# Neighbour sums: one hand-over for four tiles instead of one for each, DMA landings relayed by ScalarE, and twelve products of zeros a group instead of sixteen

## What is computed

```python
def _gin_conv(x, src, dst, n, W1, b1, gamma, beta, W2, b2):
    agg = jax.ops.segment_sum(x[src], dst, num_segments=n)
    h = x + agg
    h = jax.nn.relu(_batchnorm(h @ W1 + b1, gamma, beta))
    return jax.nn.relu(h @ W2 + b2)
```

## Time and profile before

| | us |
|---|---|
| median of 3 runs | 7083.55 (7080.03 to 7084.12) |
| the profiled execution | 7078.6 |
| its span, first to last instruction | 7076.8 |
| first call of the helper, first DMA issue to end of the last add | 568.9 to 1140.6 |
| second call | 1237.7 to 1806.7 |
| third call | 6047.9 to 6622.5 |
| mean granted TensorE clock, whole span | 0.866 of 2.4 GHz |

### The profile page before, as it was taken

One profiled execution on the slowest core, in us unless ns is written; L12 is line 12 of the kernel. 1 busy time (PEld: TensorE's weight loads), 2 busy tenths in 40 slices (PEclk: granted clock), 3 DMA queues, 4 the chain that ended last, 5 costly groups with the idle time before them and its releaser, 6 DMA issues. The chain is left out here.

```text
span 7076.8 us, 95209 instructions
## 1 busy us (share of the span) xinstructions
PE 5214.7 (74%) x22994; PEld 3478.6 (49%) x22995; DVE 3522.3 (50%) x8494; ACT 1483.9 (21%) x3917; POOL 3388.5 (48%) x3530
## 2 busy tenths in 40 slices
PE   2767886888586788677852995799987459788645
PEld 0114554555334333366642884588864334455434
DVE  7994444444445566666662112566656232444312
ACT  0001002000232677611121221333333011000111
POOL 1636773777100676577733655366620110677222
PEclk8998998999797899878775997899998559999777
DMA  4103332333100000133321774233320223333245
GB/s 160 45 17 98 103 103 65 103 104 104 29 5 16 8 2 1 25 95 94 94 47 62 232 220 139 74 107 107 107 57 0 75 73 128 105 102 103 42 152 168
DMA packets 402836, 597.07 MB, mean 84 GB/s; under 512 B 130985, under 2 KB 305641, under 8 KB 401577
## 3 DMA queue, kind: packets, MB, share of 16 engines
q0 software_dynamic: 147584, 361.63, 18.9%
q1 hardware_dynamic: 255018, 232.69, 11.1%
HBM read 472.89 MB, written 121.17 MB: 84 GB/s over the span
## 5 line engine op out<-in xcount | busy, mean ns | idle before, releaser
L644 PE MATMUL ps<-wide 128*128 128x256 f32 x2640 | 906.5, 425 | 267.5 <-DMA wide<-table,src 139.1
L629 POOL DMA_INDIRECT wide<-table,src x880 | 855.6, 972 | 506.5 <-ACTq L94 239.1
L671 DVE TENSOR_TENSOR sums<-sums,ps 128x256 f32 x1320 | 555.4, 421 | 986.6 <-PE ps L644 982.8
L641 PE MATMUL ps<-zerow,zerob 128*128 128x256 bf16 x5280 | 797.6, 274 | 44.7 <-DVE wide L125 44.7
L644 PEld LDWEIGHTS ps<-wide 128*128 128x128 f32 x2640 | 396.1, 189 | 572.1 <-DMA wide<-table,src 375.4
L641 PEld LDWEIGHTS ps<-zerow,zerob 128*128 128x128 bf16 x5280 | 519.0, 98 | 269.6 <-DVE wide L125 46.3
L629 POOL DMA_INDIRECT wide<-table_rel,rel x440 | 431.3, 980 | 351.7 <-ACTq L94 218.0
L1569 POOL DMA_INDIRECT wide<-table_gat,work x440 | 492.1, 1118 | 179.3 <-issue 133.4
L2192 POOL DMA_INDIRECT work<-table,work x440 | 441.1, 1003 | 234.7 <-issue 123.0
L1453 POOL DMA_INDIRECT work<-table_max,work x440 | 440.0, 1000 | 175.2 <-issue 111.2
L1472 PE MATMUL ps<-wide,work 128*128 128x512 f32 x880 | 479.0, 627 | 0.0
(11 more groups left out here) (433 smaller groups left out, 9864.5 us busy)
## 6 DMA issues: line engine op xcount, KB each, us to landing
wide<-in_L_ffn_W SPq DMA_DIRECT2D x64, 1024.0 KB, 6.0
wide<-in_L_ffn_expert_w SPq DMA_DIRECT2D x90, 256.0 KB, 3.1
table_rel<-wide SPq DMA_DIRECT2D x20, 1024.0 KB, 4.4
work<-rows_in SPq DMA_DIRECT2D x62, 256.0 KB, 5.5
rows_out<-work SPq DMA_DIRECT2D x62, 256.0 KB, 5.7
work<-rec SPq DMA_DIRECT2D x110, 136.0 KB, 2.1
wide<-table,src POOLq DMA_INDIRECT x880, 2.8
rec<-work POOLq DMA_DIRECT2D x6, 2176.0 KB
```

The lines of the kernel that those rows point to most:

```text
L629: nc.gpsimd.indirect_dma_start(rows[:, w % RT, :], None, table, bass.IndirectOffsetOnAxis(ap=index[:, w:w + 1], axis=0)).then_inc(gathered ...
L641: nc.tensor.matmul(m.PS[:, w % (2 * Q), 0:D], m.zerob[:, 0:P], m.zerow[:, 0:D], start=True, stop=True)
L644: nc.tensor.matmul(m.PS[:, w % (2 * Q), 0:D], S[:, w % RT, :], rows[:, w % RT, :], start=True, stop=True).then_inc(summed, 1)
L671: v.tensor_tensor(at, at, m.PS[:, s, 0:D], ALU.add).then_inc(added, 1)
```

## The change

Three things change in `aggregate`. First, the hand-overs are per group of Q = 4 tiles: POOL waits for a group of products, PE increments `summed` with the fourth product of a group, and a new semaphore `taken`, which DVE increments behind the fourth add, frees the banks. Second, PE no longer waits for DMAs. ACT waits for the four DMAs of a group and then increments `landed`, for which PE waits once. Third, the products of zeros stand once ahead of each group, and there are 12 instead of 4 times 4.

```diff
-        BEFORE = 4
+        BEFORE = 12
 ...
             for w in range(WT):
-                if w >= RT:
-                    pool.wait_ge(summed, w - RT + 1)
+                if w >= RT and w % Q == 0:
+                    pool.wait_ge(summed, (w - RT) // Q + 1)
 ...
+        @block.scalar
+        def _(act):
+            for q in range(WT // Q):
+                for w in range(q * Q, (q + 1) * Q):
+                    act.wait_ge(gathered[w % RT], w // RT * 16 + 16)
+                act.sem_inc(landed, 1)
 ...
-                if w >= 2 * Q:
-                    pe.wait_ge(added, w - 2 * Q + 1)
-                for k in range(BEFORE):
-                    nc.tensor.matmul(m.PS[:, w % (2 * Q), 0:D], m.zerob[:, 0:P], m.zerow[:, 0:D], start=True,
-                                     stop=True)
-                pe.wait_ge(gathered[w % RT], w // RT * 16 + 16)
-                nc.tensor.matmul(m.PS[:, w % (2 * Q), 0:D], S[:, w % RT, :], rows[:, w % RT, :], start=True, stop=True
-                                 ).then_inc(summed, 1)
+                if w % Q == 0:
+                    if w >= 2 * Q:
+                        pe.wait_ge(taken, w // Q - 1)
+                    for k in range(BEFORE):
+                        nc.tensor.matmul(m.PS[:, w % (2 * Q), 0:D], m.zerob[:, 0:P], m.zerow[:, 0:D], start=True,
+                                         stop=True)
+                    pe.wait_ge(landed, w // Q + 1)
+                mm = nc.tensor.matmul(m.PS[:, w % (2 * Q), 0:D], S[:, w % RT, :], rows[:, w % RT, :], start=True,
+                                      stop=True)
+                if w % Q == Q - 1:
+                    mm.then_inc(summed, 1)
 ...
                     w = k * EIGHT + s
-                    dve.wait_ge(summed, w + 1)
+                    if s % Q == 0:
+                        dve.wait_ge(summed, w // Q + 1)
                     if w:
                         dve.wait_ge(added, w)
                     at = tile_at(m.AGG, tiles[s])
                     v.tensor_tensor(at, at, m.PS[:, s, 0:D], ALU.add).then_inc(added, 1)
+                    if s % Q == Q - 1:
+                        dve.wait_ge(added, w + 1)
+                        dve.sem_inc(taken, 1)
```

More of the change, by code:

```diff
@@ L614, in aggregate @@
     with Stage(nc) as st:
-        hot, summed, added = (st.sem(s) for s in ("hot", "summed", "added"))
+        hot, summed, added, taken, landed = (st.sem(s) for s in ("hot", "summed", "added", "taken", "landed"))
         R = 8
         RT = R * Q
-        BEFORE = 4
+        BEFORE = 12
         gathered = st.sems("gathered", RT)
@@ L654, in hots @@
                 if k * EIGHT >= RT:
-                    dve.wait_ge(summed, (k + 1) * EIGHT - RT)
+                    dve.wait_ge(summed, ((k + 1) * EIGHT - RT) // Q)
                 at = k * EIGHT % RT
```

## The result

The changed kernel takes 7156.1 us (median of 5 runs, 7150.6 to 7163.0) against 7081.6 us for the kernel before: ratio 1.0106, 95% interval [1.0091, 1.0121]. That is 74.5 us slower; the prediction said 7166. The profiled execution has a span of 7158.8 us in place of 7076.8.

What follows compares the result with a forecast made beforehand. The prediction took POOL, issuing without a pause at 1.26 us a tile, to bound the calls. It summed 7078.6 + 73 (held issues) + 10 (ends of calls) = 7162 us, with the median 5 us above: 7166, range 7073 to 7212.

Steps and rivals of the forecast that it cites:

- term of +73 us: POOL's issues in the three calls: one-hot instructions hold them for 94 us in place of 21.
- offset less 0.17 us: POOL's next issue lengthens by the one-hot instruction's start behind an issue, less 0.17 us; up to about 1.09 us.
- the edge: Offset of 1.26 us behind a POOL issue, beyond which a one-hot instruction costs nothing again.
- The shift: One-hot instructions on DVE start 3.27 us later; less two POOL intervals 0.75, so the typical offset goes from 0.21 to 0.96.
- The mean over a set: POOL's loss per set of one-hot matrices: half at about 0.70 us, half spread at 0.47, mean 0.6 us.
- section on HAM oscillation: Skill text on PE: matmul bursts between DMA waits can run at half clock; by that alone every group takes 6.1 us.
- The ends: End of each call: relay, three more pairs and adds, last wait, unhidden before the barrier; 3 x 3.2 = 10 us.
- from the last product's start: Sign at a call's end: from there to the end of the last add, some 4 us instead of 1.3.
- POOL's waits at nothing: POOL's waits for PE and the ring: grouping changes nothing, the 0.30 us ahead of each issue being its own.
- No stalls: Rival: one-hot instructions start just behind a POOL issue and cost nothing; 7073, up to 7090 us; chance 0.21.
- Clock stays low: Rival: PE at 1.2 GHz needs 6.1 us a group against POOL's 5.04 and becomes the bound; 7430 us; chance 0.03.
- Faster through a shorter 0.30: Rival: POOL's 0.30 us ahead of an issue shrinks to 0.26 on 3 of 4 issues; 7033 us; chance 0.07.

Runs made afterwards that it cites:

- split kernels: Each one-hot instruction replaced by eight small ones, in the changed kernel and in the kernel before: 7067.6 and 7071.1 us on the chip with the kernel before at 7080.
- g_split_3: The changed kernel with each one-hot instruction replaced by eight on 128 x 128 with one SBUF input: 7067.6 us, 0.9986 of the kernel before.
- b_late: The kernel before with an unused DVE memset of 128 x 700 float32 ahead of each set of one-hot matrices: 7173.8 us, ratio 1.0148.

## Why the prediction was right

**Where the time goes** (term of +73 us): measured 71.5 by POOL's issues, 71.0 by its busy time (1357.9 - 1286.9). The two sides of the term were 94 and 21 us; measured 92.1 and 20.6. The rule "offset less 0.17 us" came from two sets of the kernel before. In the changed kernel it gives the extra of 151 of the 156 sets to 0.02 us, from nothing below 0.17 us to 1.05 us at an offset of 1.217. The other five, at 1.222 to 1.246 us, cost nothing. So the one thing it got wrong is the edge, which lies near 1.22 and not at 1.26. The reading of the kernel before was right too: 121 of its 156 sets stand below 0.3 us.

**The shift** (3.27 us): measured 2.95 instead of 2.83 us from the last issue of the group to the first product (relay, 0.12; taken as 0.07), 2.14 us from there to the first add (1.29 + 0.84 = 2.13), three steps of 0.56 (1.71), and 0.567 from the last add to the one-hot instruction (0.53). The sum is 3.34, which gives an offset of 1.03 us where 0.96 was said; the sets that no fall of the clock disturbed have a median of 1.01. The margin to the edge was 0.2 us and not 0.3.

**The mean over a set** (0.6 us, half of the sets at 0.70 and half at 0.47): measured 0.50, 0.59 and 0.62 in the three calls, 0.57 in all. The mechanism was right, and so was the split into halves, but the two sizes were off in opposite directions, and that they cancel is luck. In 75 sets the clock stood at its upper level while PE worked on the group ahead (taken as 5.5 to 2.0 us before the one-hot instruction). They cost 0.80 us each, since only 5 of them, and not a fifth, stand below 0.3 us. (With a fifth of them at nothing, as the prediction has it, 0.79 would have given 0.63 and not 0.70.) In the other 81 sets the clock was at its lower level for a part of that time. They are spread over all offsets, as said, but cost 0.36 and not 0.47, because 29 of them stand below 0.3 us. The clock was at its lower level 18% to 21% of the time in the calls (mean 0.89 to 0.91, said to be below 0.97), and it does stretch a group. The timeline of PE:

```profile
709.32 2.93 PE L652 MATMUL ps<-wide 128*128 128x256 f32 x6 [2.55 <-ACTq L638]
```

Six of eight records take 2.93 us here, where eight took 1.99 at 703.47. PE had idled 2.55 us, behind the held issue at 703.00. The Trainium skill's section on HAM oscillation, as the prediction cited it, is borne out in part. The clock did fall behind such waits: 88 stretches at the lower level began in the three calls, and the longest idle piece of PE just ahead of one was 2.5 us in the median. But it stayed high through most of the 227 idle pieces of 1.5 us or more, so that not every group ran at half clock. Nor did a fall cost POOL a wait: PE released it for 1.2 us in the whole first call. It acts through the phase, and at the ends.

**The ends** (10 us): 11.5 measured in the changed kernel, 9.9 between the two split kernels. The prediction looked for 4.4 us (1.26 and 3.1) "from the last product's start" to the end of the last add. Its own sum counts from the first product of the last group, since three more pairs are in it. From there it measured 5.45 us at the end of the first call, 1 us more, because the clock was low (0.64 from 1158 to 1163 us) and eight records took 3.20 us.

**POOL's waits at nothing**: right. Its 0.30 us stand ahead of the issues that have no wait as well; "PE ps L652" releases 1.2 us in the whole first call.

**The rivals.** No stalls: its shift needed 0.3 us more, or 0.26 with the edge at 1.22; it got 0.07. Clock stays low: it rose again each time. Faster through a shorter 0.30: it is 0.30 as ever.

**The rule of the Trainium skill** ("SBUF — State Buffer", "SBUF: two separate sides"), one lock for DVE and GpSimd, which a DVE instruction with two SBUF inputs takes and holds to its end, agrees with the traces in three points. An issue that starts into a one-hot instruction takes longer by the time from its own start to that instruction's end, less 0.13 us: as if it needed the ports 0.13 us behind its start and then stood still until the other had ended. The adds, with one input in PSUM, cost nothing, as the prediction said: 429 issues of the changed kernel started into an add, and none took more than 0.01 us over the usual. And the hold is for one instruction: in the split kernels no issue was held by more than 0.13 us.

The traces differ from it, or go beyond it, in two points. First, who starts first does not block the other entirely in both directions. In the changed kernel one-hot instructions that started 0.1 to 1.2 us behind the start of an issue took 1.22 to 1.23 us, as always, so the issue under way did not hold them. Second, two SBUF inputs aren't needed for the hold. The pieces of the split kernels read one SBUF tensor each, take 0.28 us (median) and start 0.20 us apart, and 144 issues of g_split_3 that started with 0.18 to 0.24 us of a piece left took 0.05 to 0.12 us longer. That is the rest of the piece less 0.13 us, the same law as for the whole instruction. So the single input does not spare POOL. What keeps the loss small is that a piece is short and that POOL gets its turn behind it; why it gets none between the memset and the one-hot instruction of b_late stays open. The pieces seem to be held in turn, unlike the whole instruction: the longest took 0.52 us, and all 100 that took over 0.40 had started 0.47 to 0.60 us behind an issue's start. DVE had room for that here. To leave the one-hot instruction whole and read one input from PSUM was not tried, since PE writes all eight banks, nor were short pieces with two SBUF inputs.

## What to carry to other kernels

When POOL issues indirect DMAs back to back, look at its busy time and its longest instructions, not only at its waits: an engine can lose time inside its instructions. A change of hand-overs that moves a long DVE instruction on SBUF against POOL's issues changes the time by its phase, even though neither engine got more work: here the price of one instruction of 1.22 us rose with the offset up to 1.05 us and then fell to nothing. Cutting that instruction into short pieces made both kernels insensitive to the phase: the held time was 10.4 us at a median offset of 1.02 us and 10.7 us at 0.21. Whether tuning the phase would do as well, no run here shows. With the pieces, grouping cost only its tail, about 3 to 4 us once per call.

## What the runs showed of the hardware that was not expected

- The hold ends sharply: in the changed kernel a one-hot instruction that started 0.039 us before an issue (offset 1.222 of 1.261) did not hold it, and one 0.044 us before it (1.217) did, for the longest time of all, 1.05 us.
- The hold goes one way for the two-input instruction: it holds an issue, and an issue under way does not lengthen it (1.22 to 1.23 us at every offset from 0.1 to 1.2 us in the changed kernel).
- Pieces with one SBUF input hold POOL by the same law, the rest of the piece less 0.13 us, and seem to be held themselves at times (0.28 us in the median, 0.52 at most, in g_split_3).
- A memset of 128 x 700 float32 on DVE, which reads nothing from SBUF, holds POOL as well, and passes the hold on to a one-hot instruction right behind it (issues of up to 2.61 us in b_late).
- On two chips indirect DMAs of 128 rows of 1 KB did not go below 1.45 us each on average over a call, against 1.26 where POOL's issuing is the bound. There the three calls of four different kernels (seven runs) lay between 1985.8 and 2004.9 us, whether POOL was busy for 1267 or for 1330 us; the fifth, with 24 zeros, took 2045.4.
